# Preparing the first attention block inside the last recurrence steps, with the last projections split by operand part and two evictions on ScalarE

## What is computed

```python
def cell(h, x):
    gi = x @ W_ih + b_ih
    gh = h @ W_hh + b_hh
    ...
    r = jax.nn.sigmoid(i_r + h_r)
    z = jax.nn.sigmoid(i_z + h_z)
    n = jnp.tanh(i_n + r * h_n)
    h_new = (1.0 - z) * n + z * h
...
q = x @ Wq + bq
k = x @ Wk + bk
v = x @ Wv + bv
scores = jnp.einsum('bdsh,bdth->bdst', q, k) / SCALE
weights = jax.nn.softmax(scores, axis=-1)
feats = jnp.einsum('bdst,bdth->bdsh', weights, v)
return feats @ Wo + bo
...
x = x + attention(gru(cond, x))
x = x + ffn(rk4(cond, cond, x))
```

## Time and profile before

| what | value |
|---|---|
| median of 3 runs | 663.62 us (660.6 to 669.09) |
| the profiled execution | 668.23 us |
| its span, first to last instruction | 666.1 us |
| mean granted TensorE clock | 0.970 |
| PE busy / weight load busy | 597.2 us (90%) / 524.3 us (79%) |
| DVE busy | 542.3 us (81%) |
| ACT busy | 396.9 us (60%) |
| POOL busy | 263.5 us (40%) |
| chain that ended last | PE 65%, DVE 24%, ACT 4%, issue 4% |

### The profile page before, as it was taken

How to read it: one execution, slowest core, us unless ns; L and a number is a source line. 1 busy time by engine, 2 the same in 40 slices (tenths; PEclk the granted TensorE clock), 3 DMA queues, 4 the chain that set the end, 5 groups by cost and what they waited for, 6 DMA issues and landing times.

```text
span 666.1 us, 13898 instructions
## 1 busy us (share of the span) xinstructions
PE 597.2 (90%) x4842; PEld 524.3 (79%) x4842; DVE 542.3 (81%) x1543; ACT 396.9 (60%) x962; POOL 263.5 (40%) x406
## 2 busy tenths in 40 slices
PE   8899999999996769997578999999999999999984
PEld 7899999999996668885466777777777777777762
DVE  3667767777766887897779999999999999999971
ACT  3554454454542434762246787878878787787764
POOL 0323323323321724312434455554545545555521
PEclk9999999999999999998779999999999999999996
DMA  8300000000000002100000000000000000000000
GB/s 288 116 3 1 1 2 1 1 2 1 1 1 17 1 1 106 66 1 1 1 0 1 9 18 10 17 17 17 10 17 17 9 17 17 17 10 17 17 18 24
DMA packets 11972, 14.85 MB, mean 22 GB/s; under 512 B 1600, under 2 KB 9344, under 8 KB 11904
## 3 DMA queue, kind: packets, MB, share of 16 engines
q1 hardware_dynamic: 11904, 13.97, 6.2%
HBM read 9.78 MB, written 4.19 MB: 21 GB/s over the span
## 4 chain that ended last, share of the span: by engine, by line
PE 65%; DVE 24%; ACT 4%; issue 4%; DMA 1%; SPq 1%; ACTq 0%; POOLq 0%; DVEq 0%
PE PS L414 21%; PE PS L306 16%; PE PS L324 12%; PE PS L470 5%; PE PS L485 3%; DVE q_s L923 3%; DVE h_s L913 2%; PE PS L392 2%; DVE h_s L1006 2%; DVE big L786 2%; PE PS L370 2%; DVE PS L881 2%; DVE q_s L937 2%; DVE PS L913 1%; ACT big L556 1%
## 5 line engine op out<-in xcount | busy, mean ns | idle before, releaser
L414 PE MATMUL PS<-h_s 128*128 128x128 f32 x1408 | 191.0, 285 | 15.1 <-DVE PS L881 7.0
L414 PEld LDWEIGHTS PS<-h_s 128*128 128x128 f32 x1408 | 171.2, 195 | 27.4 <-DVE PS L886 10.8
L306 PE MATMUL PS<-part 128*128 128x256 f32 x924 | 119.9, 287 | 3.0 <-DVE part L737 3.0
L306 PEld LDWEIGHTS PS<-part 128*128 128x128 f32 x924 | 113.8, 193 | 3.2 <-issue 3.2
L608 ACT ACTIVATE h_s<-h_s 128x128 f32<-128x128 f32 x256 | 69.0, 304 | 75.6 <-DVE h_s L913 48.1
L324 PE MATMUL PS<-big,wrk 128*128 128x128 f32 x744 | 88.4, 275 | 4.6 <-DVE big L733 4.6
L324 PEld LDWEIGHTS PS<-big,wrk 128*128 128x128 f32 x744 | 85.8, 192 | 5.2 <-DVE big L733 5.2
L1025 POOL COPY h_s<-big 128x256 f32<-128x256 f32 x32 | 21.2, 662 | 135.0 <-DVE big L733 135.0
L913 DVE SCALAR_TENSOR_TENSOR h_s<-PS,h_s 128x128 f32<-128x128 f32 x192 | 50.2, 288 | 12.2 <-PE PS L414 5.5
L907 DVE SCALAR_TENSOR_TENSOR h_s<-PS,h_s 128x256 f32<-128x256 f32 x128 | 53.2, 416 | 0.4 <-ACT PS L609 0.2
L529 ACT ACTIVATE big<-big 128x256 f32<-128x256 f32 x32 | 13.3, 416 | 65.4 <-DVE big L712 65.4
(11 more groups left out here) (140 smaller groups left out, 1209.8 us busy)
## 6 DMA issues: line engine op xcount, KB each, us to landing
out<-q_s SPq DMA_DIRECT2D x32, 128.0 KB, 1.7
x_s<-in_xT SPq DMA_DIRECT2D x14, 256.0 KB, 6.6
k_s<-in_wgT SPq DMA_DIRECT2D x1, 832.0 KB, 6.0
k_s<-in_wuT SPq DMA_DIRECT2D x1, 832.0 KB, 7.6
k_s<-in_wih SPq DMA_DIRECT2D x3, 256.0 KB, 4.8
wrk<-in_whh SPq DMA_DIRECT2D x1, 768.0 KB, 6.9
h_s<-in_wdT SPq DMA_DIRECT2D x1, 768.0 KB, 6.4
x_s<-in_xT SPq DMA_DIRECT2D x4, 128.0 KB, 3.5
```

Source lines behind the costliest of these rows:

```text
L306: r = pe.matmul(p, y, x, start=i == 0, stop=i == len(passes) - 1)
L414: return pe.matmul(PS[:, m, 0:128], w, x, start=False, stop=True, skip_group_check=True)
```

## The change

The change does six things. (1) `wv_hi` and `wv_lo` are made on VectorE at the start of steps 30 and 31. (2) The evictions of the `qk` units of steps 30 and 31 move from before L729 to behind the new state. (3) The four last units run their 16 matmuls with `h_hi` as soon as `h_hi` is there, and the 8 with `h_lo` afterwards. (4) The two last k units are evicted by ScalarE, which has a semaphore of its own for that, and `v_hi[0]` is made by ScalarE; before that it does a one-column exponential, so that the table load stands there. (5) GpSimd clears its buffers after `s_hlo31` and no longer after the last eviction. (6) `wo_hi` is made by ScalarE in block 0 and `wo_lo` by VectorE in block 1, between L769 and L773.

```diff
@@ tensor
+            pe.wait_ge(s_hi, T)
             for u in last:
-                bulk_unit(u)
+                w, m = divmod(u[2], 2)
+                ms = slice(m * 128, (m + 1) * 128)
+                slot_free(pe, u)
+                for k in range(2):
+                    for y in (wqk_lo, wqk_hi):
+                        pe.matmul(bulk_bank(u), raw(y[:, w, k, ms]), raw(h_hi[1][:, k, :]), start=k == 0 and y is wqk_lo,
+                                  stop=False)
+            pe.wait_ge(s_hlo, T - 1)
+            pe.wait_ge(s_hlo31, 1)
+            for u in last:
+                w, m = divmod(u[2], 2)
+                for k in range(2):
+                    r = pe.matmul(bulk_bank(u), raw(wqk_hi[:, w, k, m * 128:(m + 1) * 128]), raw(h_lo[1][:, k, :]),
+                                  start=False, stop=k == 1)
+                r.then_inc(s_bulk, 1)
...
-                    pe.wait_ge(s_qk, 64)
+                    pe.wait_ge(s_qk, 62)
+                    pe.wait_ge(s_qka, 2)
@@ scalar, behind the loop over steps
+            ac.wait_ge(s_const, 1)
+            ac.activation(wsum[:, 3:4], ones[:, 0:1], ACT.Exp)
+            ac.wait_ge(s_hb, T)
+            ac.activation(raw(v_hi[0]), h_s[:, :, 0:512], ACT.Copy).then_inc(s_vs0, 1)
+            for u in last[2:]:
+                kind, j, i = u
+                dst = k_s[:, i % 2, :].rearrange("p (b t) -> p t b", t=T)[:, 2 * j:2 * j + 2, :]
+                ac.wait_ge(s_bulk, number[u] + 1)
+                ac.activation(dst, bulk_bank(u).rearrange("p (t b) -> p t b", t=2), ACT.Identity,
+                              bias=ba[:, 1, i % 2:i % 2 + 1]).then_inc(s_qka, 1)
@@ scalar, block loop, behind keep_values(i, 1)
+                    if i == 0:
+                        ac.wait_ge(ld_wo, 16)
+                        ac.activation(raw(wo_hi), wo_s, ACT.Copy).then_inc(s_wo, 1)
@@ vector, start of a step
+                if t == T - 2:
+                    ve.wait_ge(ld_wv, 16)
+                    ve.wait_ge(s_bulk, number["gi", 15, 5] + 1)
+                    ve.tensor_copy(raw(wv_hi), wv_s[:, :, :]).then_inc(s_wv, 1)
+                if t == T - 1:
+                    ve.wait_ge(s_wv, 1)
+                    ve.tensor_tensor(raw(wv_lo), wv_s[:, :, :], wv_hi, ALU.subtract).then_inc(s_wv, 1)
@@ vector, end of a step
-                if n == 15:
-                    for u in qks:
-                        qk_out(u)
                 ve.wait_ge(s_so, t + 1)
...
-                if t == T - 1:
+                if t < T - 1:
+                    for u in qks:
+                        qk_out(u)
+                else:
                     hi, lo = (a[1][:, :, B:2 * B] for a in (h_hi, h_lo))
+                    qk_out(qks[0])
                     ve.wait_ge(s_hi, T)
                     ve.tensor_tensor(raw(lo), hn, hi, ALU.subtract).then_inc(s_hlo31, 1)
-                if n < 15:
-                    for u in qks:
-                        qk_out(u)
+                    qk_out(qks[1])
@@ vector, behind the loop over steps
-            for u in last:
+            for u in last[:2]:
                 qk_out(u)
-            ve.wait_ge(ld_wv, 16)
-            ve.wait_ge(s_bulk, number[last[-1]] + 1)
-            ve.tensor_copy(raw(wv_hi), wv_s[:, :, :]).then_inc(s_wv, 1)
-            ve.wait_ge(s_wv, 1)
-            ve.tensor_tensor(raw(wv_lo), wv_s[:, :, :], wv_hi, ALU.subtract).then_inc(s_wv, 1)
-            ve.wait_ge(s_hb, T)
-            ve.tensor_copy(raw(v_hi[0]), h_s[:, :, 0:512]).then_inc(s_vs0, 1)
             ve.wait_ge(s_vs0, 1)
             ve.tensor_tensor(raw(v_lo[0]), h_s[:, :, 0:512], v_hi[0], ALU.subtract).then_inc(s_vs0, 1)
-            ve.wait_ge(ld_wo, 16)
-            ve.tensor_copy(raw(wo_hi), wo_s).then_inc(s_wo, 1)
-            ve.wait_ge(s_wo, 1)
-            ve.tensor_tensor(raw(wo_lo), wo_s, wo_hi, ALU.subtract).then_inc(s_wo, 1)
...
+                if i == 1:
+                    ve.wait_ge(s_wo, 1)
+                    ve.tensor_tensor(raw(wo_lo), wo_s, wo_hi, ALU.subtract).then_inc(s_wo, 1)
@@ gpsimd
-            po_.wait_ge(s_qk, 64)
+            po_.wait_ge(s_hlo31, 1)
+            po_.wait_ge(s_hlo, T - 1)
             po_.wait_ge(s_hb, T)
```

More of the change, by code:

```diff
@@ L196, in build @@
         s_hi, s_hb, s_hlo, s_hlo31 = sem("s_hi"), sem("s_hb"), sem("s_hlo"), sem("s_hlo31")
-        s_bulk, s_gi, s_qk = sem("s_bulk"), sem("s_gi"), sem("s_qk")
+        s_bulk, s_gi, s_qk, s_qka = sem("s_bulk"), sem("s_gi"), sem("s_qk"), sem("s_qka")
         s_wv, s_vs0, s_wo, s_zero, s_vhi, s_split = (
@@ L297, in bulk_unit @@
                         pe.wait_ge(s_wqk, 2)
-                    pe.wait_ge(s_hlo, min(2 * a + 2, T - 1))
-                    if a == 15:
-                        pe.wait_ge(s_hlo31, 1)
+                    pe.wait_ge(s_hlo, 2 * a + 2)
                     ms = slice(m * 128, (m + 1) * 128)
@@ L551, in keep_scores @@
                     ac.wait_ge(s_sm, i)
-                else:
-                    ac.wait_ge(s_hb, T)
                 ac.wait_ge(s_S, i + 1)
@@ L1044, in gpsimd @@
                     po_.tensor_copy(raw(hi), src).then_inc(s_vhi, 1)
+                    if i == 0:
+                        po_.wait_ge(s_bulk, number[last[-1]] + 1)
                     po_.wait_ge(s_vhi, i + 1)
```

## The result

The changed kernel takes 660.56 us (median of 20 runs, 658.41 to 664.21), the kernel before 666.97 us (median of 20 runs beside them, 660.6 to 671.14). The ratio is 0.9922, 95% interval 0.9899 to 0.9945: faster by 5.2 us by the ratio (3.7 to 6.7) and by 6.4 us by the medians, which is under 2% but clear of no change. The forecast was 653.5 us with a gain of 10.1, so the way was right, the gain came to between half and two thirds, and the time lies just outside the stated range, 648.5 to 660. Half of the distance of 7 us between 653.5 and 660.56 is the base: the prediction started from the median of three runs, 663.62, and allowed 2 us for that; 20 runs have 666.97, 3.35 us more. The other half is missing gain, and that is what the experiments are about.

The account below looks back on a forecast made before the run. TensorE bounds up to step 30, then a VectorE-ScalarE loop, then VectorE until block 3 (255.54 us). Gains of 1.4 + 1.5 + 5.9 + 1.3 = 10.1 us, taken off the median 663.62, gave 653.5 us, range 648.5 to 660.

Parts of the forecast that it names:

- Part 1: Steps 30 and 31: without evictions between L724 and L729, 1.90 us less 0.5 us of costs, net 1.4 us earlier.
- Part 2: Last state to scores: 1.5 us gained, from 0.5 start, 0.95 clock and 0.1 eviction.
- The earlier start: Hand-over: the first 16 matmuls wait for the rounding alone, so TensorE starts at +0.55 instead of +1.06 us.
- Part 3: First blocks: 5.9 us from late or slow VectorE instructions, another 1.3 us from TensorE's clock.
- What follows it keeps its pattern: Behind the move of scores of block 3: the pattern and the weight loads were taken to stay as they were.
- rival (a): GpSimd wins against L777 in block 1, which ends 2.4 us late; gain 7.7, time 655.9, chance 0.16.
- 24 take 3.35 instead of 4.30 us: Last units in the hand-over: 24 matmuls at full clock, 0.95 us gained.
- I expect full clock: Hand-over: with about 1.9 us of idling left, TensorE was expected to keep full clock in the last units.
- another 1.3 us that should go: TensorE reaches the projection without a gap, so L392 and L358 run at full clock: 1.3 us gained.
- rival (b): TensorE's clock falls anyway in both places: 2.25 us less gained, time 655.8, chance 0.10.
- (c): Waits only move: late k evictions, or engines catching each other out in blocks 1 and 2; gain 5, 658.6, chance 0.12.
- (d): Order of L777 and L1046 turns in every block 0 to 5; 663.9, slower by 0.3, chance 0.03.

Follow-up runs that it names:

- g4: Kernel before with one wait keeping GpSimd's subtraction behind VectorE's multiplication, a second profile of it; 661.94 us profiled, no ratio.
- h1: Kernel before with extra matmuls, 20 in the hand-over and 25 ahead of the projection of block 0; ratio 1.0002.
- h2: h1 with, in addition, extra matmuls at the start of the second recurrence; 665.26 us, ratio 0.9989.
- h3: Changed kernel with 12 extra matmuls in the hand-over, those at the second recurrence's start, and the wait of e2; 658.24 us, ratio 0.9879.
- g1: Kernel before, no edit, profiled again; 669.65 us, no ratio.
- g2: Kernel before, no edit, profiled once more; 670.5 us, no ratio.
- f4: Changed kernel with 12 extra matmuls in the hand-over, between the units of step 31 and the last four units; ratio 0.9932.
- h4: Changed kernel with the last four units whole, six matmuls each behind h_lo, as before the change; ratio 0.9924.
- e2: Changed kernel with one wait more: GpSimd's subtraction for the block after next waits for VectorE's multiplication of the present block; 660.45 us, ratio 0.9904.
- e1: Changed kernel again, no edit; 659.68 us, ratio 0.9889.
- e4: Changed kernel with eight one-column activations on ScalarE ahead of the recurrence, into columns nothing reads; ratio 0.9907.
- f1: Kernel before, no edit, a second profile of it; 669.58 us, no ratio.
- e3: Kernel before with the same one wait as e2; ratio 1.0003.
- f2: Kernel before with evictions of steps 30 and 31 behind the state and `wv_hi`, `wv_lo` made in these steps, nothing else; ratio 1.0004.
- f3: Kernel before with only `wo_hi` and `wo_lo` moved into blocks 0 and 1; ratio 1.0033.

## Why the prediction was wrong

**Part 1** held: 1.4 us forecast, 1.41 measured (136.52 to 135.11). `wv_lo` was slowed by GpSimd to 0.94 us as said; `wv_hi` cost nothing that can be seen.

**Part 2** was forecast at 1.5 us and came to 1.30 in the profile. By its terms: the clock is 1.2 of it (6.09 against 4.91 us for the old hand-over at full clock, in g4 and h1), and only 0.1 is the change's own (4.91 to 4.79). The earlier start came (+0.5 us), but I put the last eviction at 0.6 us behind TensorE and it came 1.0 us behind (the scores 1.14): all units end together, and ScalarE's two evictions take 1.20 us (L564), not twice 0.47. `v_hi[0]` on ScalarE took 1.05 us, just under the forecast. The table load took 1.28 us (211.91 to 213.19), and the next instruction started at 213.20. In the Trainium skill, "ScalarE: Activation LUTs", section "What ACT_TABLE_LOAD costs", the 2.7 us that the prediction quotes are a load of 1.28 us and a drain of 1.38 us together; the load agrees with this trace, and there is no time for a drain in it.

**Part 3** was forecast at 7.2 us (5.9 and 1.3) and came to 7.34. Under the covers of h2 and h3 it is 6.1 (32.43 against 26.31 us). Up to block 3 the sum of 10.1 us came to 10.05 us between the two first profiles. g1 and g2, with the longer half clock in the hand-over, are 11.3 us longer than the changed kernel up to there.

**The steps that failed** are two, and the base. The first is "What follows it keeps its pattern". From block 3 to block 7 the first profile after took 44.86 us and not 41.81, since L797 of block 4 lost its turn. That happened in three of the five profiles that have the late exponential and not the wait (the first, f4, h4), for 3.0, 1.7 and 3.1 us, some 1.5 us in the mean. It is the mechanism of rival (a), in block 4 and not in block 1: a margin of 0.27 us that I took from the earlier trace rows was eaten by a lateness of 0.28, and the two starts now lie within 0.02 us. This step is shown in the traces. What it costs in the mean is not, since e2 has no such turn and the same time.

The second is the one that took the clock's falls as a fixed cost of the kernel before and as gone in the changed one: "24 take 3.35 instead of 4.30 us" with "I expect full clock" in part 2 and "another 1.3 us that should go" in part 3, 2.25 us together. I had read them in one execution. For the changed kernel it is shown that this fails at one of the two places: in three of six profiles without cover in the hand-over the clock fell in the last units all the same (e1, e4, h4: 6.1 to 6.6 us to the scores), which cost 1.5 us in e1 and 1.3 in e4. That is rival (b) at one place; 2.02 us of idling did not settle it.

For the kernel before it is likely and not shown. All four profiles of it have both falls. Only g4, which has one wait more, had neither: its fall came in block 0, which cost it some there (the moves of scores of blocks 0 and 1 are 10.5 us apart instead of 7.9), and from the last state to block 3 it was 4.9 us shorter than the first profile before, so the change gains 5.2 us over it and not 10.0. Of 84 timed executions of the kernel before, those with a mean clock of 0.965 to 0.973 fall into 5 of 660.9 to 661.9 us and 26 of 666.2 to 670.7, and the profiled executions of it (668.23, 669.58, 669.65, 670.5) are all of that upper band. The 17 with 0.962 lie between 663.1 and 665.7, the others from 661.8 to 673.7. The execution that the sum was read from was thus longer than most, but where the shorter ones save their time no trace of the plain kernel shows.

**A third cost lies behind the attention**, and the prediction has no term for it. From the move of scores of block 7 to the end the profiles without extra matmuls at the start of the second recurrence take:

| kernels | profiles | us |
|---|---|---|
| before, plain | first, f1, g1, g2 | 368.7, 368.7, 368.6, 368.6 |
| before, variants | e3, f2, g4, f3, h1 | 370.5, 370.5, 366.9, 366.3, 366.1 |
| changed and its variants | first, e1, e2, e4, f4, h4 | 368.6, 370.2, 370.7, 370.6, 370.8, 370.6 |

The means are 368.3 for the nine before and 370.2 for the six changed. Much of it is the start of the second recurrence: its first two steps take 26.5 to 26.9 us, with the clock at half for some 24 us, in five of the six changed and in two of the nine before, and 23.9 to 24.9 us otherwise. Whether the change brings this about or these executions happened to have it, no run tells; if it holds in the mean, it takes 1.9 us of the gain.

Put together, the gain in the sum's stretches is 5.2 us over g4, 10.1 over the first profile before and 11.3 over g1 and g2. The costs to be taken off are some 1.5 us for the turn of block 4, some 0.7 us for the last units (half of the profiles, 1.4 us each) and up to 1.9 us behind the attention. From the first profile before they leave 6.0 to 7.9 us, against 6.4 by the medians of 20 and 7.8, 4.4 and 4.6 by those beside e1, f4 and h4. So two accounts fit: the execution that was priced was one of the long ones, or its gain was real and is taken back behind block 3. The pieces are shown in single profiles; how they share the missing gain in the mean stays open.

The base is the other half of the miss, and there the sum used an allowance of 2 us where 3.35 were needed.

**The rivals.** (c), that the waits only move within blocks 1 and 2, did not happen. (d) did not either: one block turned, not six. (a) and (b) each came about in part and in some executions; I had priced each as if it held always or never.

**What stays open.** e2 takes the lost turn of block 4 away and is no faster than the changed kernel (660.45 against 660.56), though the 1.5 us are at the edge of what its interval can tell. In the kernel before, e3 gains 2.4 us up to block 3 and f2 2.0 in the trace, and neither shows in 12 timed runs; why is not known. What happens behind the last step of the second recurrence differs too (29.9 to 32.4 us). No profile of the plain kernel before in its lower band was caught, and no run has the kernel before at full clock throughout its first blocks.

## What to carry to other kernels

Take a second profile before pricing a stretch by its clock: what one execution shows as a fall in one stretch may stand in another in the next, and a gain counted there may be had in some executions alone. Where two engines exclude each other, the distance between their starts is a number like any other: a margin as small as an engine's lateness (here 0.27 us against 0.28) is no order. A wait made it one and took the lost turns out of the traces, though no gain showed in the timed runs. Extra matmuls that are to cover idle time must be checked for whether the engine still idles when its next work is released; in h1 it did not. A base of three runs that spread by 8 us can miss the median by more than half of what the change is worth (3.35 of 6.4 us here).

## What the runs showed of the hardware that was not expected

- The half level of TensorE's clock came after idling of 1.95 us (block 4 of the first profile after) and did not come after 3.04 us (g4). The length of the idling just ahead did not decide it here.
- An extra 0.28 us without any wait ahead of ScalarE's exponential of block 4 is in seven of eight profiles of the changed kernel and its variants, always at the same instruction (0.37 us from the subtraction instead of 0.10), and moves to an earlier one, the move of scores of block 4, when eight instructions are added ahead (e4).
- Started within 0.02 us of each other, VectorE's and GpSimd's two-operand instructions still exclude each other: VectorE's took 0.69 and GpSimd's 2.91 us in e1, where both started at 262.98, and GpSimd's 2.36 and VectorE's 2.90 us in h4, where GpSimd's was 0.02 us ahead. The Trainium skill, "SBUF — State Buffer", section "Who interferes with whom", has the rule that the one issued first goes first; the trace agrees in h4 at a distance of 0.02 us, and in e1 the starts do not tell which was first.
- A slower TensorE went with a faster VectorE: the values of block 0 at half clock (2.93 instead of about 1.7 us) held GpSimd back and won the turn for L777 (1.13 instead of 2.21 us, in h1).
